# A fused attention and feed-forward block: order of score and maximum tiles, turning blocks and normalizing pieces changed

## What is computed

```python
x = x + tanh(g_xattn) * attention(layernorm(x), ctx, mask)   # 4 x 1024 tokens, width 512, 16 heads of 32
x = x + tanh(g_ffn)   * ffn(layernorm(x))                    # int8-style quantized, 512 -> 2048 -> 512, GELU
# attention:
Q, K, V = projections                                       # of 4 x 16 heads, 1024 queries, 1024 keys
scores = Q @ K^T / sqrt(32);  scores[mask == 0] = -1e9
attn = softmax(scores);  ctx = attn @ V;  out = ctx @ Wo^T + bo
```

## Time and profile before

| what | value |
|---|---|
| runs | 1655.22, 1659.69, 1660.45 us (median 1659.69) |
| the profiled execution | 1657.17 us, span 1655.4 us |
| PE busy | 1423.1 us, 86% of the span, 14598 matmuls |
| DVE busy | 1313.9 us, 79% |
| POOL busy | 932.0 us, 56% |
| ACT busy | 865.7 us, 52% |
| mean granted TensorE clock | 0.962 of full |

### The profile page before, as it was taken

The page is one execution under the profiler, slowest core; times in us unless marked ns, Lnnn a source line. Parts: engine busy times, 40 slices in busy tenths (PEclk is TensorE's granted clock), DMA queues, the critical chain, the costliest instruction groups (busy, mean ns, idle before and its releaser), DMA issues. The chain is left out here.

```text
span 1655.4 us, 36545 instructions
## 1 busy us (share of the span) xinstructions
PE 1423.1 (86%) x14598; PEld 576.1 (35%) x14598; DVE 1313.9 (79%) x1337; ACT 865.7 (52%) x932; POOL 932.0 (56%) x693
## 2 busy tenths in 40 slices
PE   4899999569999899989998999999978938993998
PEld 1344444223333333333333333333323414441433
DVE  7777776488888788878887788888826997999786
ACT  3233223136666566656665666666661347872553
POOL 7131111057777677777777677777773749920011
PEclk9899999789999999999999999999998968996999
DMA  8565563832033303321331233030006805562886
GB/s 280 143 217 187 165 217 125 221 104 61 28 82 78 68 25 84 76 54 41 84 74 42 54 84 75 21 75 21 11 24 229 304 26 204 242 259 109 289 297 227
DMA packets 126917, 207.07 MB, mean 125 GB/s; under 512 B 11956, under 2 KB 65204, under 8 KB 125248
## 3 DMA queue, kind: packets, MB, share of 16 engines
q1 hardware_dynamic: 119616, 187.73, 36.6%
q0 software_dynamic: 3424, 8.95, 1.7%
q10 hardware_dynamic: 3744, 8.39, 1.4%
HBM read 124.29 MB, written 72.35 MB: 119 GB/s over the span
## 5 line engine op out<-in xcount | busy, mean ns | idle before, releaser
L724 POOL TENSOR_TENSOR x<-x 128x512 f32<-128x512 f32 x512 | 670.0, 1321 | 220.3 <-ACT x L765 213.3
L792 DVE TENSOR_REDUCE row_max<-ring 128x1 f32<-128x1024 f32 x512 | 617.1, 1219 | 153.1 <-PE ring L626 146.7
L765 ACT ACTIVATE x<-ring 128x1024 f32<-128x1024 f32 x512 | 514.7, 1027 | 317.2 <-PE ring L688 317.2
L650 PE MATMUL o_acc<-x,v 128*32 128x512 f32 x2048 | 265.9, 596 | 3.0 <-ACT x L765 3.0
L626 PE MATMUL ring<-ffn_w_int 128*32 128x512 f16 x2560 | 194.9, 381 | 13.4 <-DVE row_max L792 13.2
L688 PE MATMUL ring<-ffn_w_int 128*32 128x512 f16 x2560 | 181.5, 382 | 22.7 <-issue 10.5
L626 PE MATMUL ring<-x 128*32 128x512 f16 x1536 | 118.9, 392 | 31.9 <-DMA v<-scratch_V 16.8
L659 PE MATMUL sum_acc<-x,ones 128*32 128x512 f32 x1024 | 132.1, 592 | 0.6 <-POOL x L724 0.6
L1361 PE MATMUL down<-ffn_w_int,hq 128*128 128x512 bf16 x512 | 114.8, 385 | 14.9 <-ACT hq L1347 14.9
L1152 PE MATMUL hid<-xqT,ffn_w_int 128*128 128x512 bf16 x512 | 119.1, 389 | 8.7 <-ACT xqT L1182 7.6
L688 PEld LDWEIGHTS ring<-ffn_w_int 128*32 128x32 f16 x2560 | 60.2, 96 | 179.4 <-issue 70.9
(11 more groups left out here) (181 smaller groups left out, 2079.0 us busy)
## 6 DMA issues: line engine op xcount, KB each, us to landing
scratch_G<-gelu SPq DMA_DIRECT2D x56, 512.0 KB, 2.6
g_in<-scratch_G SPq DMA_DIRECT2D x28, 1024.0 KB, 6.1
x<-in_ctxT SPq DMA_DIRECT2D x8, 1024.0 KB, 7.1
x<-in_x SPq DMA_DIRECT2D x8, 1024.0 KB, 8.8
scratch_V<-x SPq DMA_DIRECT2D x32, 256.0 KB, 3.1
v<-scratch_V SPq DMA_DIRECT2D x16, 512.0 KB, 5.7
out<-x POOLq DMA_DIRECT2D x7, 1024.0 KB, 7.4
ffn_w_int<-scratch_QH SPq DMA_DIRECT2D x20, 256.0 KB, 4.0
```

Source lines behind the costliest of these rows:

```text
L650: last = nc.tensor.matmul(oacc[h * DK:(h + 1) * DK], v[buf][:, kt, h * DK:(h + 1) * DK], prob[:, s % 2, h, part], tile_position=(0, h * DK ...
L724: nc.gpsimd.tensor_tensor(pair[:, s % 2, h], prob[:, s % 2, h, 0], prob[:, s % 2, h, 1], ALU.add).then_inc(pair_done, 1)
L765: nc.scalar.activation(prob[:, s % 2, h], ring[slot][:], ACT.Exp, scale=SM_SCALE).then_inc(exp_done, 1)
L792: nc.vector.tensor_reduce(mraw[:, i:i + 1], ring[slot][:], AX.XY, ALU.max).then_inc(max_done, 1)
```

## The change

AHEAD goes from 24 to 26, so that six N units instead of eight remain and the M units begin in the middle of step 1 instead of in step 2. STEP swaps its eighth and ninth place, so that S and M alternate all through (the ring sees S M S M S M S M). The turns X and Y are put behind the second maximum of steps 6 and 2 instead of behind the second score. Of the normalizing pieces, sums_out stays at (1, 0), the inversion goes to (2, 0), normalize to (2, 2), low to (3, 2); on ACT, take_out is one exponential later and `high` moves from (2, 1) to (3, 0), three exponentials later. SP's and POOL's lists are the same in both.

```diff
-        AHEAD = 24
+        AHEAD = 26
         OWN = MU - AHEAD
-        STEP = "SMVSMVSSMVM"
+        STEP = "SMVSMVSMSVM"
...
                 if kind == "S":
                     out.append(("S", GH * step + i))
+                elif kind == "M":
+                    m = GH * step + i
+                    out.append(("N", AHEAD + m) if m < OWN else ("M", m - OWN))
                     if i == 1 and step == TURN_OWN:
                         out.append(("Y", 1))
                     if i == 1 and step == TURN_NEXT:
                         out.append(("X", 0))
-                elif kind == "M":
-                    m = GH * step + i
-                    out.append(("N", AHEAD + m) if m < OWN else ("M", m - OWN))
...
-                        if (s, h) == (KP, 2):
+                        if (s, h) == (KP, 3):
                             take_out(0, t)
-                        if (s, h) == (0, 2) and not first:
+                        if (s, h) == (0, 3) and not first:
                             take_out(1, t - 1)
-                        if (s, h) == (KP + 2, 1):
+                        if (s, h) == (KP + 3, 0):
                             high(0, t)
-                        if (s, h) == (2, 1) and not first:
+                        if (s, h) == (3, 0) and not first:
                             high(1, t - 1)
...
-            AFTER = {(1, 0): sums_out, (1, 1): invert, (1, 2): normalize, (2, 3): low}
+            AFTER = {(1, 0): sums_out, (2, 0): invert, (2, 2): normalize, (3, 2): low}
```

More of the change, by code:

```diff
@@ L539, in stage_attend @@
         FROM = -len(PREPARE) % RING
-        assert len(RINGED) % RING == 0 and OWN % GH == 0 and OWN // GH <= TURN_OWN
+        assert len(RINGED) % RING == 0 and OWN <= GH * TURN_OWN and OWN + MU // 2 <= GH * TURN_NEXT
         def head_and_tile(i):
```

## The result

The changed kernel takes 1599.91 us in the median of four runs (1597.31 to 1603.38), the kernel before 1657.78 us in four (its three and one more beside them). The ratio is 0.965, 95% interval 0.963 to 0.967: 3.5% faster. The profiled execution took 1599.11 us, span 1597.3.

The account below looks back on a forecast made before the run. PE was taken to bound the kernel, losing 3.0 us per half waiting for ring buffers. Fifteen groups at -3.6 us, last group -2 and prologue +2.3 gave -53.7, perhaps -56, from 1657.17: 1603 us, range 1590 to 1622.

Parts of the forecast that it names:

- Half a group: Four steps and a turn in mid-attention: 24.4 us of PE work plus 1.2 of waits, 25.6 instead of 27.39.
- The waits: PE per half: a score 0.08, the turn 0.05, third maximum of step 6 0.62, score behind o_lo 0.47; together 1.22 us.
- minus_max_cols and o_lo: DVE operations beside POOL's additions in each half: minus_max_cols about 0.3 to 0.4 us, o_lo 1.39.
- o_norm: DVE piece starting 12.68 us into the half, with POOL's addition ending at 12.89: 0.77 us.
- the first rival: DVE's pieces meet POOL at its worst: all three 1657 to 1662 us, 3%; o_norm alone 1629, 9%.
- The take-out: ACT's copy moves behind the step's fourth exponential: costs nothing, and the 0.54 us per half is gone.
- Plain steps at 6.04: Under strict alternation a plain step of PE takes 6.04 us, without the 0.2 of maxima too close for DVE.
- Last group -2, prologue +2.3: Last group saves 2.3 us, -2 taken; the prologue makes 26 maxima before the first score, +2.3 us.
- Loop rounds at 0: PE's three pauses between the loop's four rounds, 3.46 us in one case, stay: 0, within 1 us each.
- First group: Its halves may gain a little more from starting with no pieces, which could make the total -56 us.
- Rival 2: Queued maxima take DVE 1.22 us instead of 1.13: 52.2 us per group, 1618 us in all; chance 5%.
- Rival 4: Maximum rows come late and first scores of halves wait: 1690 us if the landing took 8.5 us; chance 2%.

Follow-up runs that it names:

- e2_order: The kernel before with the new STEP string alone: 1640.30 us, ratio 0.991.
- e11_take: The kernel before with the take-out alone one exponential later: 1644.03 us against 1657.69, ratio 0.993.
- e8_low_last: The changed kernel with o_lo alone one maximum later, at (3, 3): 1601.57 us, ratio to before 0.967.
- e4_later: The changed kernel with inversion, o_norm and o_lo each one maximum later: 1588.27 us, ratio to before 0.960.
- e12_unrolled: The kernel of e4_later with SP's loads in three portions and the twelve looped groups written out: 1565.17 us, ratio to before 0.943.
- e10_low_spread: The kernel of e8_low_last with SP's loads for group t+2 issued in three portions: 1593.09 us, ratio to before 0.960.

## Why the prediction was right

The range (1590 to 1622) held the time, 1603 was 3 us above the median of 1599.91. Between the two profiled executions the change is 58.1 us, where the sum had 53.7 to 56; the terms below say where the rest is. The mechanism held: which operation waits for which, and where.

- **Half a group**: 25.6 predicted, 25.51 measured. The waits: 0.08, 0.05, 0.62, 0.47 predicted (1.22), 0.06, 0.13, 0.42, 0.06, 0.47 measured (1.14; the fourth, a score at 684.14, was not foreseen). The third was over-priced by 0.2: the inversion held DVE for 0.91 instead of 1.00 and the maximum behind it took 1.19 instead of 1.22, and PE itself came 0.07 later.
- **minus_max_cols and o_lo**: 0.3 to 0.4 and 1.39 predicted, 0.38 and 1.36 measured. This was the least certain step, since no operation stood in these places before, and it came right from following POOL's additions beside DVE's.
- **o_norm**: 0.77 predicted, 0.93 in most halves, since it began 0.1 us earlier and the addition ended 0.1 later than thought, and 1.2 to 1.4 in a few (421.58: 1.37, 630.55: 1.36, these two right behind a pause of PE). A milder form of the first rival, with o_norm alone, happened there, in about four halves of 31; these are 0.3 to 0.8 us longer, PE's pause included where there was one.
- **The take-out**: its wait is gone, as predicted, but the text gave the reason as the move of the copy; e2_order and e11_take show that either edit alone does it.
- **Plain steps at 6.04**: right where DVE has no extra work: steps 3 and 7 take 6.03 us in the thirteenth and fourteenth group after the first, and 6.08 in most looped ones.
- **Last group -2, prologue +2.3**: -1.7 and +2.3 (the first score 33.55 us after the first maximum instead of 31.29).
- **Loop rounds at 0**: they cost 10.7 us over the regular pace instead of 14.4. A gain of 3.7 that the sum didn't have, partly given back in the odd halves (2.3), so here two errors offset each other.
- **First group**: said to bring perhaps a little more; the stretch from the first score to the second transpose gained 3.1.
- **Rival 2** (queued maxima at 1.22) didn't happen: in the changed kernel two queued maxima take 2.36 us, so they start 1.14 apart. **Rival 4** didn't: no score waited for max rows, the longest landing was 3.4 us.
- **What the prediction didn't have**: TensorE short of instructions. It cost little here; it did break the same kind of sum for e8_low_last, where 4 to 7 us were expected and none came.

## What to carry to other kernels

When two engines share buffers in a short ring, write down for one period where each buffer is given back and put every extra operation of the busier reader between two units whose distance has room; the regular halves worked out ahead for the orders tried here were right within 0.15 us, but for e4_later (0.25). The time of nine of the twelve runs came within 3 us of what was written ahead; e4_later (5), e8_low_last (6) and e12_unrolled (5) did not. The DVE instructions here whose duration varied at constant size were waiting inside: look at what the neighbour engine runs at that instant before counting such time as work. And when an engine comes within a few per cent of its limit, look at "issue" idle: a burst of loads that cost nothing before can stop it then, and the loop's rounds, which cost 14 us from the start, are a larger part of what is left.

## What the runs showed of the hardware

- Work of GpSimd that bounds nothing costs DVE time: additions of 512 columns (1.28 us) against 256 (0.73) changed minus_max_cols from 1.16 to 0.60 us in one kernel and o_lo from 1.36 to 0.81 in the other, and the kernels by 24 and 17 us. The waiting lies inside DVE's record: minus_max_cols ends 0.06 us behind the addition that it met, o_norm and o_lo 0.55.
- Beside a burst of some 2.6 MB of loads in 12 us, instruction packets came 12 to 16 us apart instead of 8.4, and PE stopped for 0.3 to 1.5 us (e8_low_last); with the same loads in three portions there is no such pause, and the kernel is 8.5 us faster (e10_low_spread).
- A round of the hardware loop cost PE a pause of 2.4 to 3.9 us, 2.4 to 7.9 with what follows, and writing twelve groups out gave 16.7 us. The Trainium skill, Runtime: NRT & Kernel Launch, section "Instruction fetch mechanics", says that a taken branch out of the fetched window stalls until a DMA has brought the target's page; the trace agrees (3.46 us at a round, none in e12_unrolled).
- A weight load's wait for a buffer rose by half (71.5 to 110.4 us) while the kernel got 3.5% faster: this row of the list of waits is no measure of PE's loss.
